# The memory of lines in a three-block network: order of the work over eight tiles, and ScalarE takes part of the state update

## The reference, cut to what matters

```
w1, w2, r1, r2 = projections of x (4 numbers per head; w1 of the token before)
write_lines = exterior(w1, w2)          # 6 products of pairs, divided by their norm
read_lines  = exterior(r1, r2)
Jw    = write_lines @ J6
outer = Jw[..., :, None] * Jw[..., None, :]                 # 6 x 6 per token and head
M_all = decayed cumulative sum of outer over the earlier tokens, per head
rd_M  = einsum('bhti,bhtij->bhtj', read_lines, M_all)
score_M, score_M2 = sum(rd_M * read_lines), sum(rd_M * rd_M)
mem_score = (1 - alpha) * score_M + alpha * score_M2
out = (softmax attention + mean_h(sigmoid(mem_score * scale) * gate) * mem_val) @ out_w.T + out_b
```

## Time and profile before

| what | us |
|---|---|
| median of 3 runs (lowest, highest) | 1924.51 (1923.56, 1925.54) |
| the profiled execution's own time | 1925.14 |
| its span, first to last instruction | 1923.4 |
| PE, DVE, ACT, POOL busy in it | 1856.9, 1604.4, 1490.7, 920.7 |

### The profile page before, as it was taken

How to read it: one execution, slowest core, us unless ns; L and a number is a source line. 1 busy time by engine, 2 the same in 40 slices (tenths; PEclk the granted TensorE clock), 3 DMA queues, 4 the chain that set the end, 5 groups by cost and what they waited for, 6 DMA issues and landing times. The chain is left out here.

```text
span 1923.4 us, 61311 instructions
## 1 busy us (share of the span) xinstructions
PE 1856.9 (97%) x22646; PEld 1107.9 (58%) x22646; DVE 1604.4 (83%) x5459; ACT 1490.7 (78%) x4110; POOL 920.7 (48%) x552
## 2 busy tenths in 40 slices
PE   7999999999999989999999999889999999999999
PEld 3777774577775343433344347637777635777754
DVE  5999974899995668999999949979999658999945
ACT  4999994699998362777777764469999847999973
POOL 2788861488882050000000035548888505888820
PEclk8999999999999996999999999999999999999999
DMA  5212130122221041111111000002121201121311
GB/s 178 52 44 50 44 70 6 29 50 45 50 53 39 1 153 36 42 42 42 42 42 42 25 6 3 2 20 50 44 51 44 62 6 36 44 50 44 69 23 44
DMA packets 76522, 85.33 MB, mean 44 GB/s; under 512 B 17423, under 2 KB 51027, under 8 KB 76099
## 3 DMA queue, kind: packets, MB, share of 16 engines
q1 hardware_dynamic: 76031, 81.40, 17.0%
q10 hardware_dynamic: 196, 0.02, 0.0%
HBM read 20.83 MB, written 8.39 MB: 15 GB/s over the span
## 5 line engine op out<-in xcount | busy, mean ns | idle before, releaser
L336 ACT ACTIVATE probs<-probs,negmax 128x128 f32<-128x128 f32 x1024 | 401.8, 402 | 1.6 <-DVE negmax L411 1.0
L2334 ACT ACTIVATE gprobs<-ps_global 128x1024 f32<-128x1024 f32 (+3 forms) x384 | 291.5, 811 | 125.9 <-PE ps_global L1765 103.2
L291 POOL TENSOR_TENSOR rot<-rot 128x1024 f32<-128x1024 f32 x128 | 302.3, 2362 | 144.8 <-DVE rot L381 144.8
L297 POOL TENSOR_TENSOR qk<-rot,cnorm 128x1024 f32<-128x1024 f32 x128 | 243.8, 1905 | 172.8 <-issue 149.0
L304 POOL TENSOR_TENSOR probs<-probs,iden 128x1024 f32<-128x1024 f32 x128 | 242.8, 1897 | 46.6 <-DVE iden L419 46.0
L2010 DVE TENSOR_REDUCE maxes<-ps_global 128x1 f32<-128x512 f32 (+2 forms) x384 | 221.9, 636 | 11.5 <-PE ps_global L1728 6.5
L411 DVE CUSTOM_DVE_ANT_0 probs<-ps_attn,masks 128x128 f32<-128x128 f32 x1024 | 226.0, 284 | 0.6 <-issue 0.5
L1723 PE MATMUL ps_global<-kq 48*128 48x512 bf16 (+3 forms) x768 | 197.4, 346 | 7.0 <-DVE maxes L2010 1.8
L336 ACT ACTIVATION_READ_ACCUMULATOR probs<-probs,negmax 128x1 f32 x1024 | 203.9, 199 | 0.0
L2251 POOL CAST m_parts<-m_turn 32x128 bf16<-32x128 f32 x16 | 4.5, 280 | 364.6 <-DVE m_turn L2024 364.6
L377 DVE TENSOR_TENSOR rot<-ps_attn,rotary 128x512 f32<-128x512 f32 x256 | 174.7, 682 | 3.1 <-PE ps_attn L202 2.6
(11 more groups left out here) (235 smaller groups left out, 4489.7 us busy)
## 6 DMA issues: line engine op xcount, KB each, us to landing
v_first<-v_second SPq DMA_DIRECT2D x256, 128.0 KB, 2.3
hs<-z_a SPq DMA_DIRECT2D x256, 32.0 KB, 1.9
ln<-z_b SPq DMA_DIRECT2D x56, 128.0 KB, 2.4
kq<-split_scratch SPq DMA_DIRECT2D x64, 96.0 KB
kq<-split_scratch SPq DMA_DIRECT2D x64, 64.0 KB
split_scratch<-parts SPq DMA_DIRECT2D x8, 384.0 KB, 4.3
split_scratch<-gprobs SPq DMA_DIRECT2D x6, 384.0 KB, 4.0
x_tok<-in_x_dram SPq DMA_DIRECT2D x4, 512.0 KB, 5.9
```

Of the source, the lines that this page charges most:

```text
L291: nc.gpsimd.tensor_tensor(a, a, b, ALU.add).then_inc(C["rot_sum"], 1)
L297: nc.gpsimd.tensor_tensor(qk[:, k % 2, :].rearrange("p (h d) -> p h d", d=DH), rot_a[:, k % 2, :, :], cnorm[:, k % 2, :].unsqueeze(2).to_b ...
L336: last = nc.scalar.activation(probs[:, k % 2, slot, :], probs[:, k % 2, slot, :], ACT.Exp, scale=-1.0, bias=negmax[:, k % 2, slot:slot + 1 ...
L2334: nc.scalar.activation(probs[:, step % RING, 2 * p:2 * p + 2, 0:w], ps[:, S0 + 2 * p:S0 + 2 * p + 2, 0:w], ACT.Exp).then_inc(C["p2_exp"], 1)
```

## The change

It does these things:

- DVE: the second clip of a tile moves from the end of the body that makes it into the next body, behind the first `multiply` and the first part of the terms. Multiplies 6 and 7 come ahead of the second `read_memory`, and that ahead of the first `sum_squares`; the second `sum_squares` comes last, behind `advance`.
- POOL: `outer_products(t + 1)` comes ahead of the second normalisation of tile t + 1, which is now in the same body instead of the one before.
- ACT: the decay of the state (`fade`, four activations with a scale per partition) is new, and `advance` for k > 0 becomes two additions of 288 columns (the faded state in SBUF and the tail in PSUM). Left copies 6 and 7 come ahead of the first square. The first two left copies of the next tile come ahead of the second inverse.
- PE: `tails` comes ahead of the last part of `memory`.
- SP: the state's row is one DMA in place of four; for this, heads are assigned to partitions by j * 4 + q instead of 4 * q + j.

```diff
@@ PE
-                        h = GROUP * q + j
+                        h = GROUPS * j + q
-                    wait(pe, f"ml_row{k % 2}", 16 * GROUP * (k // 2 + 1))
+                    wait(pe, f"ml_row{k % 2}", 16 * (k // 2 + 1))
                 lines(4, 6)
-                memories(5, 6)
                 if t + 1 < LAST:
                     tails(t + 1)
+                memories(5, 6)
                 lines(6, 8)
@@ DVE
-                wait(dve, f"ml_row{(k + 1) % 2}", 16 * GROUP * ((k + 1) // 2))
+                wait(dve, f"ml_row{(k + 1) % 2}", 16 * ((k + 1) // 2))
+                if k > 0:
+                    wait(dve, "ml_faded", k)
+                    for half in range(2):
+                        at = slice(half * GROUPS // 2, (half + 1) * GROUPS // 2)
+                        last = nc.vector.tensor_tensor(state[:, (k + 1) % 2, at, :].rearrange("p q n -> p (q n)"),
+                                                       faded[:, at, :].rearrange("p q n -> p (q n)"),
+                                                       ps[:, TAIL_BANKS[half], 0:2 * STATE_ROWS], ALU.add)
+                    last.then_inc(C["ml_state"], 1)
+                    return
...
                 multiplies(0, 1)
                 all_terms(0, 1)
+                if 1 < t + 1 < S_TILES:
+                    clip(t + 1, 1)
                 multiplies(1, 2)
...
                 all_terms(5, 6)
+                multiplies(6, 8)
+                if valid(t):
+                    read_memory(t, 1)
                 if valid(t + 2):
                     sum_squares(t + 2, 0)
-                if valid(t):
-                    read_memory(t, 1)
-                multiplies(6, 8)
                 if valid(t):
                     weigh(t)
                 if valid(t + 2):
                     clip(t + 2, 0)
-                    sum_squares(t + 2, 1)
                 if t + 1 < LAST:
                     advance(t + 1)
                 if valid(t + 2):
-                    clip(t + 2, 1)
+                    sum_squares(t + 2, 1)
@@ POOL
                 if valid(t + 1):
                     outer_products(t + 1)
+                    normalise(t + 1, 1)
                 if valid(t + 2):
                     subtract(t + 2, 0)
                     subtract(t + 2, 1)
                     normalise(t + 2, 0)
-                    normalise(t + 2, 1)
@@ ACT
+            def fade(k):
+                wait(act, "ml_state", k)
+                for q in range(GROUPS):
+                    last = nc.scalar.activation(faded[:, q, :], state[:, k % 2, q, :], ACT.Identity, scale=A["whole"][:, q:q + 1])
+                last.then_inc(C["ml_faded"], 1)
...
-                lefts(0, 2)
+                if t == 0:
+                    lefts(t, 0, 2)
                 if valid(t - 2):
                     copy_scores(t - 2)
-                lefts(2, 5)
+                if 0 < t + 1 < LAST:
+                    fade(t + 1)
+                lefts(t, 2, 5)
                 if valid(t):
                     scale_lines(t)
-                lefts(5, 6)
+                lefts(t, 5, 8)
                 if valid(t + 2):
                     square_line(t + 2, 0)
-                lefts(6, 8)
-                if valid(t + 2):
                     inverse(t + 2, 0)
                     square_line(t + 2, 1)
+                lefts(t + 1, 0, 2)
+                if valid(t + 2):
                     inverse(t + 2, 1)
@@ SP
-                for j in range(GROUP):
-                    sp.dma_start(outer[TILE - 1:TILE, k % 2, j:AH:GROUP, :], state[32 * j:32 * j + 1, k % 2, :, :]
-                                 ).then_inc(C[f"ml_row{k % 2}"], 16)
+                sp.dma_start(outer[TILE - 1:TILE, k % 2, :, :].rearrange("p (j q) n -> p j (q n)", j=GROUP),
+                             state[0:P:32, k % 2, :, :].rearrange("j q n -> j (q n)")).then_inc(C[f"ml_row{k % 2}"], 16)
```

More of the change, by code:

```diff
@@ L1560, in global_attention_pass @@
             "ml_outer", "ml_tail", "ml_state", "ml_row0", "ml_row1", "ml_m", "ml_term", "ml_read", "ml_plain", "ml_blend", "ml_weight",
-            "ml_score", "ml_turned", "ml_out"))
+            "ml_score", "ml_turned", "ml_out", "ml_faded"))
     U2 = P2_STEPS
@@ L1585, in global_attention_pass @@
         den_late = sb("den_late", [P, 2 * CHUNK // AH])
+        faded = sb("faded", [P, GROUPS, B * LINE * LINE])
         ps = ctx.enter_context(nc.psum_tensor(C.own("ps_global"), [P, 8, CHUNK], F32))
@@ L2419, in body, with lefts @@
             def body(t):
-                def lefts(first, end):
+                def lefts(t, first, end):
                     if valid(t + 2):
@@ L2744, in sync_decay @@
         for j in range(GROUP):
-            sp.dma_start(A["whole"][32 * j:32 * j + 1, :], decay[0:1, j:AH:GROUP, TILE], allow_slow_non_contiguous=True
+            sp.dma_start(A["whole"][32 * j:32 * j + 1, :], decay[0:1, GROUPS * j:GROUPS * (j + 1), TILE], allow_slow_non_contiguous=True
                          ).then_inc(C["as_row"], 16)
```

## The result

| kernel | median us (lowest, highest) | runs |
|---|---|---|
| before | 1924.53 (1923.56, 1925.54) | 4 |
| after | 1954.89 (1953.51, 1955.39) | 4 |

The ratio is 1.0155, 95% interval 1.0143 to 1.0167. The change costs 30.4 us; forecast were 17.2, in a range of 1923 to 1946. The sign and the held clip came out as written; the size did not, because a second cost had no term in the sum. One run of experiment 7's kernel, 2115.63 us at a mean granted clock of 0.841 (0.981 to 0.984 in its other three), is in the slow state and stands outside every comparison. The profiled execution took 1955.39 us with a span of 1953.6; I forecast 1942.3 for it, so 13.1 are missing in the sum.

A forecast was written before the change was run, and what follows sets the result against it. DVE was taken to set the pace, closely followed by PE. Terms -0.6 before the loop, +0.43 body 0, +16.17 bodies 1 to 5, +1.17 bodies 6 and 7 sum to +17.2 us: forecast 1941.7, range 1923 to 1946.

The forecast's parts named there:

- The hold: DVE's second clip, begun inside POOL's outer product, waits for that product's end: 2.9 us a body; chance 0.70.
- (a): Rival: the clip runs beside the outer product without a hold, body 13.19 us, total level at 1924.4; chance 0.14.
- (b): Rival: no hold, and PE's path shorter than read, so DVE's own work decides: -12.1 us, 1912.4; chance 0.10.
- the 0.25: Sign that one-input DVE instructions also hold POOL: its copy beside DVE's takes 0.86 us, its cast elsewhere 0.61.
- Multiply 1 at 3.88: In DVE's loop body, the clip is released at 3.8 us, so multiply 1 starts at 3.88, where it was 0.78.
- 4.84 behind multiply 7: DVE's work from multiply 7 to the next body takes 4.84 us after the change, where it was 4.41.
- The four fades: Four new scalings of the state on ACT, ahead of left copies 2 to 4: 1.4 us in all, bounds 0.8 and 2.1.
- Item 7's left is ready 7.35 later: PE's unbroken row and ACT's copy let multiply 7 start 7.35 us after multiply 1, giving a body of 16.07.
- PE idle about 3 us a body before item 3: Sign expected in the changed profile: PE pauses about 3 us in each body before its projection of item 3.
- Bodies 6 and 7, +1.17: At the loop's end the last tile's held clip makes PE begin tile 7's products at about 9.75, not 8.58: +1.17 us.
- Level without the hold, 1924.4: Total if the clip were not held: the body's other gains and losses together -0.1 us, giving 1924.4.
- Below this no gain, above it no loss: PE's tails ahead of the last product: the fifth product comes 1.1 us later for DVE, which waits for item 6 anyway.

The follow-up runs named there:

- experiment 7: Kernel after, with only POOL's outer products put back behind the second normalisation, the late clip staying in the next body: 1934.57 us, ratio 1.0057.
- experiment 1: Kernel after, with only the second clip moved from behind the first terms to behind the first half of the reads: 1925.61 us, 0.9997 of before.
- experiment 2: Kernel after, with ACT writing the late inverse of tiles 2 to 7 to PSUM and the clip reading it there: 1926.93 us, ratio 1.0011.
- experiment 4: Kernel before, with one unused 64-column SBUF-to-SBUF clip added on DVE behind terms 1 and 2 in bodies 1 to 5: 1939.14 us, ratio 1.0066.
- Experiment 3: Kernel after, with nine unused 192-column matmuls added on PE between items 2 and 3 of bodies 1 to 5: 1943.27 us, ratio 1.0087.
- experiment 5: Kernel of experiment 1, with the second read put back ahead of multiplies 6 and 7: 1921.86 us, ratio 0.9987.
- experiment 6: Kernel of experiment 5, with sum of squares and advance ahead of weighing behind multiply 7, and the late clip behind terms 5: 1920.39 us, ratio 0.9971.

## Why the prediction was right in kind and wrong in size

- **The hold: right.** Forecast 2.9 (2.7 to 3.1 in the profile), measured 3.11 or 3.12, and 2.81 in body 2, where the reciprocal stands ahead of the clip. Experiments 1, 2 and 4 leave nothing of rivals (a) and (b) for this order. A clip ahead of the loop (at 1133.54) was held for 2.86 too, which I had not seen coming; DVE had time there. One of the reasons for the hold was weak: the 0.25 by which POOL's copy (0.86) exceeds its cast (0.61) compares two operations, and all four such copies of the kernel before take 0.86, each beside DVE's copy and none alone.
- **Multiply 1 at 3.88: right** (3.92), and **4.84 behind multiply 7: right** (4.85), with the weight product at 0.56 and the two additions at 0.73 start to start (taken as 0.74). The four fades take 1.33 (taken as 1.4).
- **"Item 7's left is ready 7.35 later": the step that failed.** I took the row from a trace in which PE never paused and the granted clock was 1.00, and set it behind a pause of 3 us that my own list of signs names ("PE idle about 3 us a body before item 3"). After that pause TensorE gets a clock near the lower of its two levels, 1.2 instead of 2.4 GHz (0.55 in the 3.8 us behind it, 0.83 over the five bodies), and from multiply 1 to multiply 7 it takes not 7.35 but 10.26, 9.30, 8.81, 10.25 and 9.30 us in bodies 1 to 5. That is 11.2 us above five times 7.35, of the 11.35 by which the five bodies are longer than forecast. Experiment 3 fills the pause and finds 16.06 in body 3. The range had no term for it either: its upper end summed latencies and the advance, and ended at 1946.
- **Bodies 6 and 7, +1.17: too small by 2.7, the same step.** PE begins tile 7's products 12.59 us into this stretch (1267.47), where I had 9.75. Ahead of them the gates take 1.73 more, start to start (3.57 against 1.84), and eight memory matmuls take 2.21 where fourteen took 1.92 before, about 1.1 more by an estimate from these two rows. Together that is about the 2.84 missing. No experiment fills the pauses of body 6: that the clock makes this part is argued from the rows and the 0.76, not shown by a run of its own.
- **Level without the hold, 1924.4: right** (1925.61 in experiment 1, 1926.93 in experiment 2), for the reason given: 1.58 us of work were moved out of PE's shadow. Experiments 5 and 6 move the read back.
- **Tails first, "Below this no gain, above it no loss": right only with an early product and while item 7 decides.** Experiment 7 shows the price without the early product, and in experiment 6 the last memory part, behind the tails, makes one of the two waits left (0.61).

The Trainium skill, "TensorE: Matmul & The Clock Gate", section "HAM oscillation — how this bites in real kernels", describes a kernel in which every wait for a DMA lets the engine fall back to the slow clock, so that the cost is paid each time. The windows of the kernel after show the same pattern for a pause that VectorE makes (0.83 over bodies 1 to 5), and the 11.6 us of experiment 3 are its price here. The page's waits are those of another kernel: it raises the question of a second term, and that the pause of this kernel is enough for it is shown by the windows alone.

## What to carry to other kernels

An instruction of 0.2 us on VectorE can cost 3 us if it lies inside a long GpSimd product and works from SBUF to SBUF; put it outside, or let it read PSUM. When a forecast makes TensorE pause for some microseconds in every round of a loop, every duration of TensorE that was read from an unbroken row is no longer good for the work behind the pause: price it at the lower clock as the upper bound. Before work is moved behind the last input of a round, ask what it was lying beside.

## What the runs showed of the hardware

- The `tensor_scalar` of 64 columns, float32, SBUF to SBUF, one input: 0.18 us alone, 3.12 when it begins 0.96 into a GpSimd `tensor_tensor` of 4.03, 0.22 there when its input is in PSUM. The additions, products and terms with one PSUM input ran beside GpSimd at their usual times (0.60 for 432 columns at 1200.52, inside the product; 0.81 for the two additions at 1216.64, beside the normalisation).
- The instruction's recorded duration contains the wait, so VectorE looked busy: 3.90 of 3.92 us in the window that holds the clip. Busy time alone would not have shown it; the duration against that of the same form elsewhere does.
- In the kernel after, matmuls without any use in the pause brought the granted clock of bodies 1 to 5 from 0.83 to 1.00 and made it 11.6 us faster.
